# A first-block step table with weight loading, rounding and testing as steps of their own

## The reference

```
x = x + tanh(g_xattn) * attention(layernorm(x), ctx, ctx)      # 16 heads of 16, causal mask,
                                                              # softmax(q k^T / 4), then Wo and bo
x = x + tanh(g_ffn) * ffn(layernorm(x))
ffn(x):  h = silu((x @ w1.T) * w1_s) * ((x @ w2.T) * w2_s)    # 256 -> 1024
         h = gelu((h @ h1.T) * h1_s)                          # 1024 -> 1024
         h = gelu((h @ h2.T) * h2_s)                          # 1024 -> 1024
         return (h @ w3.T) * w3_s                             # 1024 -> 256
```

## Time and profile before

| | |
|---|---|
| median of 3 runs | 1783.74 us (1782.88 to 1784.28) |
| the profiled execution's own time | 1783.53 us |
| its span | 1781.2 us |
| busy share of the span | PE 97%, DVE 74%, ACT 74%, POOL 62% |
| first FFN matmul (end of turn 0's work) | 82.61 us after the start of the span |

### The profile page before, as it was taken

One profiled execution on the slowest core, in us unless ns is written; L12 is line 12 of the kernel. 1 busy time (PEld: TensorE's weight loads), 2 busy tenths in 40 slices (PEclk: granted clock), 3 DMA queues, 4 the chain that ended last, 5 costly groups with the idle time before them and its releaser, 6 DMA issues.

```text
span 1781.2 us, 39684 instructions
## 1 busy us (share of the span) xinstructions
PE 1721.5 (97%) x11078; PEld 1471.0 (83%) x11078; DVE 1319.0 (74%) x2803; ACT 1310.2 (74%) x3022; POOL 1098.3 (62%) x1647
## 2 busy tenths in 40 slices
PE   4599999999999999999999999999999999999998
PEld 3488888888888888888888888888888888888886
DVE  4877777777777777777777778777787777777763
ACT  3778777778777778777777777777777777777773
POOL 3567656667656667656657655656755656765652
PEclk7699999999999999999999999999999999999999
DMA  8644444444444544444544444444344454444420
GB/s 298 202 121 112 121 130 135 141 131 113 115 135 130 147 132 114 114 132 131 142 143 111 118 127 135 137 141 115 115 123 135 135 141 121 115 124 130 118 60 7
DMA packets 362523, 229.29 MB, mean 129 GB/s; under 512 B 274688, under 2 KB 332288, under 8 KB 360960
## 3 DMA queue, kind: packets, MB, share of 16 engines
q1 hardware_dynamic: 360336, 217.14, 43.4%
q10 hardware_dynamic: 2160, 11.81, 1.7%
HBM read 113.53 MB, written 41.94 MB: 87 GB/s over the span
## 4 chain that ended last, share of the span: by engine, by line
PE 92%; issue 2%; DMA 1%; DVE 1%; ACT 1%; POOL 1%; SPq 1%; POOLq 0%; ACTq 0%; DVEq 0%
PE ffn L984 71%; PE work L924 13%; PE s_bank L959 3%; PE pv L975 3%; PE work L1064 2%; SPq L357 0%; DMA q_saved<-q_parts 0%; DMA aw<-in_attn_w 0%; DMA xT<-in_x_T 0%; POOL hb L516 0%; ACT probs L824 0%; SPq L361 0%; DMA k_saved<-k_parts 0%; DVE full L654 0%; POOL ha L511 0%
## 5 line engine op out<-in xcount | busy, mean ns | idle before, releaser
L984 PE MATMUL ffn<-hb,W 128*128 128x512 f32 x2048 | 504.3, 399 | 1.3 <-POOL hb L516 1.3
L661 DVE TENSOR_REDUCE full<-ffn 128x256 f32<-128x512 f32 x512 | 349.5, 688 | 180.1 <-PE ffn L984 175.7
L984 PE MATMUL ffn<-ha,W 128*128 128x512 f32 x2048 | 479.9, 391 | 1.2 <-POOL ha L511 1.2
L984 PEld LDWEIGHTS ffn<-ha,W 128*128 128x128 f32 x2048 | 378.0, 188 | 80.9 <-POOL ha L511 2.4
L984 PEld LDWEIGHTS ffn<-hb,W 128*128 128x128 f32 x2048 | 375.2, 188 | 82.1 <-POOL hb L516 8.8
L824 ACT ACTIVATE probs<-probs,exp_bias 128x128 f32<-128x128 f32 x1024 | 320.3, 390 | 42.6 <-POOL exp_bias L479 41.5
L471 POOL TENSOR_TENSOR p_parts<-probs,p_parts 128x512 f16<-128x512 f32 x256 | 299.1, 1168 | 20.5
L984 PE MATMUL ffn<-x2T_hi,W 128*128 128x256 f32 x1024 | 260.2, 290 | 1.0 <-DVE x2T_lo L757 0.5
L516 POOL TENSOR_TENSOR hb<-full,hb 128x256 fp32r<-128x256 f32 x256 | 187.8, 739 | 112.4 <-ACT full L842 104.8
L984 PE MATMUL ffn<-x2T_lo,W 128*128 128x256 f32 x1024 | 254.3, 284 | 0.0
L842 ACT ACTIVATE full<-full,cols 128x256 f32<-128x256 f32 x512 | 253.2, 494 | 0.0
(11 more groups left out here) (86 smaller groups left out, 2432.5 us busy)
## 6 DMA issues: line engine op xcount, KB each, us to landing
k<-k_saved SPq DMA_DIRECT2D x256, 128.0 KB, 2.7
q<-q_saved SPq DMA_DIRECT2D x256, 128.0 KB, 2.7
k_saved<-k_parts SPq DMA_DIRECT2D x32, 512.0 KB, 2.9
q_saved<-q_parts SPq DMA_DIRECT2D x32, 512.0 KB, 2.9
wnat<-in_ffn_w ACTq DMA_DIRECT2D x11, 1024.0 KB, 6.4
xT<-in_x_T SPq DMA_DIRECT2D x32, 256.0 KB, 3.3
cT<-in_ctx_T SPq DMA_DIRECT2D x32, 256.0 KB, 3.4
x_in<-in_x SPq DMA_DIRECT2D x32, 256.0 KB, 3.6
```

Source lines behind the costliest of these rows:

```text
L661: dve.tensor_reduce(full[:, m % 4], src[:].rearrange("p (a t) -> p t a", a=2), AX_X, ALU.add).then_inc(done, 1)
L984: return pe.matmul(dst, w, h, **flags)
```

## The change

W.k is taken apart: G.k on ACT issues the load of chunk k, W.k on ACT rounds it, C.k on DVE tests it. Each has its own place in the list; no load stands ahead of turn 0 any more. The load of `aw` is cut in two: wq and wk first, then cT and x, then wv and woT, for which V of block 0 waits (`value_w_in`). And the list `PROLOGUE` is another one throughout. The main list `ORDER` is as it was. Line numbers above 400 are 1 to 3 higher in the changed kernel.

```diff
@@ -32,12 +32,13 @@
 
 
 PROLOGUE = steps("""
-    Q.0 k q.0 q.1 W.0 st i.0 W.1 v K Q.1 e.0 i.1 V W.2 S.0 kw qw e.1 S.1 W.3 kr.0 i.2 S.2 S.3 Q.0+ s.0 m.0 p.0 qr.0
...
+    G.0 st G.1 rx q.0 q.1 k Q.0 i.0 W.0 qw v K C.0 i.1 W.1 C.1 s.0 p.0 m.0 Q.1 q.0+ V s.1 G.2 i.2 e.0 Q.0+ S.0 S.1
...
+    To.0 m.7 O.0 e.5 R.3 C.7 W.5 PV.6 W.6 R.4 G.8 V+ nh.1 T.7 p.6 nm.0 G.9 PV.7 e.6 W.7 G.10 To.1 nm.1 e.7 R.5 kr.0+
...
 """)
 ORDER = steps("""
     L1.0 i.1 S.2 L1.1 L1.2 s.2 Q.0+ g.0 p.0 L1.3 l.0 lt+ L1.4 a1.0 a1.1 lc+ S.3 S.4 f.0 e.1 p.1 a1.2 l.1 L1.5 lx+
@@ -179,7 +180,7 @@
         ffn = [bank("ffn0"), bank("ffn1"), bank("ffn2")]
 
 
-        attn_w_in = sem("attn_w_in")
+        attn_w_in, value_w_in = sem("attn_w_in"), sem("value_w_in")
         scales_in = sem("scales_in")
         gates_loaded = sem("gates_loaded")
         pool_const = sem("pool_const")
@@ -405,9 +406,11 @@
                         store(n - 2)
 
             load_xT(0)
-            sp.dma_start(aw[:].rearrange("p w k e -> p (w k e)"), attn_w[:, :]).then_inc(attn_w_in, 16)
+            half = 2 * KE * E
+            sp.dma_start(aw[:, 0:2].rearrange("p w k e -> p (w k e)"), attn_w[:, 0:half]).then_inc(attn_w_in, 16)
             load_c(0)
             load_x(0)
+            sp.dma_start(aw[:, 2:4].rearrange("p w k e -> p (w k e)"), attn_w[:, half:2 * half]).then_inc(value_w_in, 16)
             body(0, ffn_on=False, weights=True)
 
             sp.wait_ge(flag_ready, 1)
@@ -682,7 +685,7 @@
                         l1_silu(j, k)
                     if kind == "f" and ffn_on:
                         l1_product(j, k)
-                    if kind == "W" and weights:
+                    if kind == "C" and weights:
 
                         dve.wait_ge(chunk_in[k % STAGES], 16 * (k // STAGES + 1))
                         wait(dve, chunk_tested, k)
@@ -789,15 +792,11 @@
             act.dma_start(cols[:].rearrange("p a m -> p (a m)"), scale_cols[:, :]).then_inc(scales_in, 16)
             act.dma_start(bo_tg[:], bo.rearrange("(a n) -> a n", a=1).partition_broadcast(P)).then_inc(scales_in, 16)
             act.dma_start(s3_tg[:], w3s.rearrange("(a n) -> a n", a=1).partition_broadcast(P)).then_inc(scales_in, 16)
-            for i in range(STAGES):
-                load_chunk(i)
             act.wait_ge(gates_loaded, 16)
             act.activation(gates[:], gates_in[:], ACT.Tanh).then_inc(gates_ready, 1)
 
             def round_chunk(i):
 
-                if i > 0 and i + STAGES - 1 < CHUNKS:
-                    load_chunk(i + STAGES - 1)
                 act.wait_ge(chunk_in[i % STAGES], 16 * (i // STAGES + 1))
                 act.activation(W[:, i * CHUNK:(i + 1) * CHUNK], wnat[:, i % STAGES], ACT.Copy).then_inc(chunk_rounded, 1)
 
@@ -864,6 +863,8 @@
                             wait(act, l1_lo, j * KF + (k - 3))
                         act.activation(full[:, k % 4], ffn[use][:, 0:TOK], ACT.Tanh, scale=half_s1[:, k:k + 1])\
                             .then_inc(tanh_ready, 1)
+                    if kind == "G" and weights:
+                        load_chunk(k)
                     if kind == "W" and weights:
                         round_chunk(k)
                     if kind == "R" and weights:
@@ -942,6 +943,8 @@
                                        lambda kt: cT[:, kt])
                     last.then_inc(k_ready, 1)
                 if kind == "V":
+                    if isinstance(n, int) and n == 0:
+                        pe.wait_ge(value_w_in, 16)
                     wait(pe, cT_loaded, (n + 1) * 16)
                     for b in range(ROWS):
                         last = project(bank_[:, b * E:(b + 1) * E], lambda kt: cT[:, kt, b * P:(b + 1) * P],
```

More of the change, by code:

```diff
@@ L34 @@
 PROLOGUE = steps("""
[L35 to L40 removed]
+    G.0 st G.1 rx q.0 q.1 k Q.0 i.0 W.0 qw v K C.0 i.1 W.1 C.1 s.0 p.0 m.0 Q.1 q.0+ V s.1 G.2 i.2 e.0 Q.0+ S.0 S.1
+    m.1 S.2 p.1 S.3 s.2 K+ kw Q.1+ m.2 p.2 T.0 i.3 G.3 S.4 p.3 s.3 lr s.4 PV.0 e.1 lt+ q.1+ S.5 G.4 T.1 C.2 qr.0 e.2
+    kr.0 T.2 PV.1 lc+ R.0 k+ i.4 T.3 m.3 m.4 kr.1 W.2 C.3 qr.1 G.5 R.1 lx+ e.3 s.5 S.6 m.5 W.3 S.7 nh.0 PV.2 C.4 G.6
+    qw+ T.4 i.5 S.0+ S.1+ PV.3 s.6 T.5 R.2 C.5 qr.0+ PV.4 p.4 p.5 st+ e.4 C.6 W.4 kw+ T.6 s.7 m.6 G.7 i.6 i.7 PV.5
+    To.0 m.7 O.0 e.5 R.3 C.7 W.5 PV.6 W.6 R.4 G.8 V+ nh.1 T.7 p.6 nm.0 G.9 PV.7 e.6 W.7 G.10 To.1 nm.1 e.7 R.5 kr.0+
+    R.6 O.1 s.0+ C.8 m.0+ nh.2 C.9 W.8 p.7 o.0 C.10 i.0+ to.0 nh.3 nm.2 nm.3 R.7 v+ F.0 o.1 n2.0 to.1 W.9 kr.1+ F.1
+    lr+ n2.1 qr.1+ W.10 x2.0 x2.1 s.1+ rx+ X2.0 X2.1 m.1+ e.0+
 """)
```

5 lines of the change are left out of this document (removed).

## The result

The changed kernel takes **1792.13 us** (median of 6 runs, 1788.74 to 1793.33) where the kernel before took 1783.55 in the same session: ratio 1.0048, 95% interval 1.0037 to 1.0059. It is 8.6 us slower; 1783.6 had been forecast, and the range ended at 1788.5. The profiled execution took 1793.33 us with a span of 1791.0 us, so it is 1.2 us over its median, and 9.8 us over the one of before.

A forecast was written before the change was run, and what follows sets the result against it. Turn 0 was taken as the bound: waits up to the first score, then DVE. First score 28.0 plus 54.5 us put L1.0 at 82.5 instead of 82.61; 1783.53 - 0.1, rounded with the median, gave 1783.6 us, range 1778.5 to 1788.5.

The forecast's parts named there:

- the main loop passes a shift on: Main loop: PE busy 52.88 of 53.00 us, so the end moves by as much as L1.0 moves.
- The first half of `aw`: Start of turn 0: half the bytes land at an estimated 5.9 us instead of 7.55; bounds 5.3 and 7.55.
- first score: S.0 on PE in turn 0: at 28.0 us, 3.4 us earlier than before; bounds 27.1 and 30.8.
- DVE's work from there to L1.0: DVE behind the first score: 40.42 us of before plus 4.58 for two moved tests, 45.0 us.
- ahead of the first mask: DVE idle between the first score and the first mask: 0.8 us, as before.
- hole ahead of the fifth mask: DVE waits for S.4, which has K+, Q.1+ and T.0 ahead of it on PE: 4.1 us.
- meetings, chunk 8, tail: DVE idle: tests meeting POOL instructions 1.5 us, chunk 8 and PV.7 ahead of nh.3 1.0, o.1 to L1.0 2.1.
- DVE is the engine to watch: First score to L1.0, 51.16 us in the kernel before: DVE was busy 40.42 us and idle 10.74.
- the landing of the last placing: Last DMA placing queries and keys ahead of the first score: lands 3.6 us after issue, between 2.7 and 6.4.
- The slower rival: Four meetings of tests and POOL on the path cost 6.0 us instead of 1.5: 1788.1 us; chance 0.23, combinations included.
- The backlog rival: Placings still land 6.4 us after issue, xT, cT and chunk 2 replacing chunk 3: first score 30.8, 1786.4 us; chance 0.12.
- The faster rival: The new list closes the holes and no meeting costs anything: L1.0 at 77.9, 4.7 us less, 1778.9 us; chance 0.31.

The follow-up runs named there:

- e8_short_tests: The changed kernel with the tests of chunks 1 to 10 cut to a sixteenth of their columns, steps and waits in place: median 1791.41 us, ratio 1.0039.

## Why the prediction was wrong

**Held.** That the main loop passes a shift on: 1698.5 us behind L1.0, 1698.6 before. The first half of `aw`, forecast for 5.9 us: the mean starts at 5.95. No wait for a chunk over 2 us: 1.00 was the longest on DVE. Casts of up to 2 us beside tests: 1.87 us at 73.33. What I had named as signs of being wrong came too: a first score past 30, and L1.0 past 86.

**The sum, term by term**, in the profiled execution (us):

| term | forecast | measured |
|---|---|---|
| first score | 28.0 | 30.41 |
| DVE's work from there to L1.0 | 45.0 | 44.63 |
| ahead of the first mask | 0.8 | 0.81 |
| hole ahead of the fifth mask | 4.1 | 5.01 |
| DVE waits for PV.3 behind S.0+ | not there | 6.66 |
| meetings, chunk 8, tail (1.5 + 1.0 + 2.1) | 4.6 | 5.0, the rest of 62.13 |
| L1.0 | 82.5 | 92.54 |

**The step that failed** is one that wasn't made: the price of PV.3's new place on PE was put at nothing, without a reason. I walked DVE's list and priced S.4 by what stands ahead of it on PE, but I never asked the same of PV.3. In the new list S.0+ stands ahead of it, and I had silently taken its keys as there when PE came by. They weren't: PE stood 11.78 us for them, and DVE 6.66 us for PV.3, which is the only new term and 6.66 of the 10.0 us by which L1.0 missed.

Asking would not have been enough. The prediction follows the new chain "by the durations of the old one", and by these the keys are in time: 49.98 plus the 8.1 us from write to S.0+ of before gives 58.1 us, when PE had finished T.4 at 57.9. In the changed kernel those 8.1 us became 19.7, since chunk loads that the change puts there run beside them; with light loads they were 9.3 (50.54 to 59.80). The landing of a DMA is the duration that can't be carried over from another traffic.

A third premise fell with `e8_short_tests`: "DVE is the engine to watch". With 17 us less of its work behind the first score, L1.0 came 0.4 us sooner (and the first score 1.2). DVE's 45.0 us came out right (44.63) and weren't what the end waited for, so the table above keeps the account of one execution and isn't a list of causes.

**The step that was mis-sized** is the landing of the last placing: 3.6 us forecast, "nearer to the first since a chunk of 1 MB is gone". Another one had come. I had G.2 issued at 24.4, together with the last placing; it was issued at 23.32 us, beside the last two (their row above), and the score came at 30.41, some 7 us after them and close to my upper bound of 30.8. The placings themselves were issued 1.3 us sooner than forecast (18.69 instead of 20.0 for the first), so the landing was off by more than the 2.4 us of the first score. With G.2 out of the way a placing took 3.2 or 3.0 us and the scores came at 27.6 and 27.3; where a slow Q.0+ held G.2 back to 24.5 us or later, they came at 28.2 to 29.2. The forecast's 28.0 held for a load that comes behind the placings.

**The rivals.** The slower rival gave 1788.1 by meetings of tests and POOL. The sign was right and the mechanism wrong. The meetings are there (and the prediction sets "a meeting at each of the nine tests" equal to this rival, which prices only four). POOL, beside tests:

```profile
53.62 3.14 POOL L474 TENSOR_TENSOR p_parts<-probs,p_parts 128x512 f16<-128x512 f32 x1
...
58.05 3.16 POOL L474 TENSOR_TENSOR p_parts<-probs,p_parts 128x512 f16<-128x512 f32 x1
```

That subtraction takes 1.16 us at 49.28. But short tests brought 0.7 to 1.6 us, which the intervals don't tell from none; a wait for the keys followed. What the meetings would cost once the keys' wait is gone was not tried. The backlog rival had its cause right (chunk 2 in the place of chunk 3) and nearly its first score (30.8; 30.41 measured), and is 2.4 us of the answer; I gave it a chance of 0.12, and where it came together with meetings the price was still that of meetings alone. The faster rival had the loads' own places as its ground, and these are a good part of what the loss is made of. The range failed because its slower end was one rival's price: two waits together weren't in it.

**How far the cause is shown.** Shown: keys late because of chunk loads (write to S.0+ 9.3 us beside light loads, 19.7 beside full ones), a loss because PV.3 stands behind them (5.4 us back by putting S.0+ and S.1+ back with their steps), the first score held by G.2 (3.7 us by the medians), and the three places together as the whole (1.0003, 0.9994 to 1.0012). The tail's share is small and its interval takes in zero. Open is why small loads with the scores back were slower than small loads alone; how much of the 5.4 us is the keys' wait and how much S.1+'s wait for its bank; whether the three gains overlap; and how often Q.0+ runs at full clock, since only one execution of each kernel has a trace.

## What to carry to other kernels

A list that is shared by all engines sets the order of each queue: for every instruction that is moved ahead, ask on its own engine what now stands behind it, and walk the chain of its operand back through the DMA queues, with latencies for the load that the change itself puts there. Work for the next block may stand ahead of the current block's only where its data is surely in. And where bulk loads get places of their own, the place beside a short transfer on the critical path is the expensive one: hold the load back until that transfer has landed.
